# Transposed maxima in the bank of the value products, and a latent softmax that is normalised behind its product with the values

## The reference, cut to what matters

```python
h = layernorm(x) * (1 + ca) + sa
q, k, v = split(h @ qkv_w + qkv_b)                 # 16 heads of 16
local = window_attention(q, k, v)                  # the 128 tokens before, softmax
pooled = h.reshape(B, 64, 16, D).mean(2)           # 64 latents, chunks of 16 tokens
rk, rv = split(pooled @ rkv_w + rkv_b)             # 4 latent heads of 16
lattn = softmax((h @ rq_w + rq_b) . rk / 4 over earlier chunks)   # 0 where there are none
remote = (lattn . rv) @ rout_w + rout_b
gate = sigmoid(local @ gl_w + remote @ gr_w)
x = x + ga * ((gate * local + (1 - gate) * remote) @ out_w + out_b)
```

## Time and profile before

| | us |
|---|---|
| median of 3 runs | 580.47 |
| lowest and highest | 572.05, 580.49 |
| the profiled execution's own time | 576.64 |
| its span, first to last instruction | 574.9 |

### The profile page before, as it was taken

One profiled execution on the slowest core, in us unless ns is written; L12 is line 12 of the kernel. 1 busy time (PEld: TensorE's weight loads), 2 busy tenths in 40 slices (PEclk: granted clock), 3 DMA queues, 4 the chain that ended last, 5 costly groups with the idle time before them and its releaser, 6 DMA issues.

```text
span 574.9 us, 19855 instructions
## 1 busy us (share of the span) xinstructions
PE 482.9 (84%) x7168; PEld 364.1 (63%) x7168; DVE 436.6 (76%) x1193; ACT 353.8 (62%) x868; POOL 379.2 (66%) x516
## 2 busy tenths in 40 slices
PE   2446689999899999999999999999999999988771
PEld 2205567777677666777777676777776676766451
DVE  2155657788688888988988788888888887878554
ACT  1210466677677667777777577777776776766540
POOL 2222346778577767788877587777777677766663
PEclk9975889999899999999999899999999999999776
DMA  9558644618244444434252607162534444440000
GB/s 277 114 133 246 163 105 99 132 47 187 56 113 75 95 94 93 94 90 93 64 101 68 119 34 145 39 125 62 120 68 97 92 94 93 82 79 10 11 10 19
DMA packets 56523, 55.15 MB, mean 96 GB/s; under 512 B 7380, under 2 KB 53100, under 8 KB 54892
## 3 DMA queue, kind: packets, MB, share of 16 engines
q1 hardware_dynamic: 53564, 52.57, 41.4%
q10 hardware_dynamic: 2864, 1.31, 1.1%
HBM read 37.07 MB, written 16.80 MB: 94 GB/s over the span
## 4 chain that ended last, share of the span: by engine, by line
PE 72%; issue 11%; POOL 5%; DVE 4%; DMA 2%; ACT 2%; ACTq 1%; SPq 1%; POOLq 0%; DVEq 0%
PE p_pv L819 9%; PE p_qkv L730 9%; PE p_qkv L740 6%; PE p_misc L886 6%; PE p_y L806 5%; PE p_x L785 5%; PE p_y L807 5%; PE p_x L778 4%; PE p_a L751 3%; PE p_qkv L860 3%; PE p_misc L869 2%; PE p_a L831 2%; PE p_a L716 2%; PE p_misc L877 2%; PE p_a L753 2%
## 5 line engine op out<-in xcount | busy, mean ns | idle before, releaser
L592 ACT ACTIVATE pr<-p_y 128x512 f32<-128x512 f32 x224 | 124.6, 595 | 55.8 <-PE p_y L807 52.9
L1159 DVE TENSOR_REDUCE mtok<-p_x 128x3 bf16<-128x480 f32 (+1 forms) x192 | 109.3, 585 | 30.9 <-PE p_x L785 29.6
L441 POOL TENSOR_SCALAR_AFFINE_SELECT pr<-pr 128x512 f32<-128x512 f32 x128 | 89.6, 701 | 11.2 <-ACT pr L594 9.0
L451 POOL TENSOR_TENSOR rstd<-ve,half 128x1 f32<-128x1 f32 x96 | 58.1, 605 | 47.9 <-DVE ve L1079 47.7
L469 POOL TENSOR_TENSOR dif<-local,rem 128x272 f32<-128x272 f32 x32 | 30.9, 965 | 83.8 <-DVE local L1197 83.8
L445 POOL TENSOR_SCALAR_AFFINE_SELECT pr<-pr 128x512 f32<-128x512 f32 x112 | 81.3, 726 | 0.0
L807 PE MATMUL p_y<-qst,kst 112*128 112x128 bf16 x512 | 73.2, 221 | 0.0
L806 PE MATMUL p_y<-qst,kst 112*128 112x128 bf16 x448 | 66.5, 221 | 7.7 <-ACT pr L592 4.8
L819 PE MATMUL p_pv<-pr,vp 128*18 128x128 f32 x1920 | 67.1, 279 | 2.1 <-POOL pr L445 0.8
L730 PE MATMUL p_qkv<-hT,wqk 128*128 128x256 f32 x256 | 66.1, 403 | 2.2 <-DVE qkf L1111 1.3
L740 PE MATMUL p_qkv<-wv,hT 128*128 128x272 f32 x128 | 40.1, 439 | 29.5 <-issue 29.4
(11 more groups left out here) (131 smaller groups left out, 1092.7 us busy)
## 6 DMA issues: line engine op xcount, KB each, us to landing
scr_q<-terms SPq DMA_DIRECT2D x16, 384.0 KB, 2.5
qst<-scr_q SPq DMA_DIRECT2D x16, 384.0 KB, 4.7
scr_k<-terms SPq DMA_DIRECT2D x16, 384.0 KB, 4.4
kst<-scr_k SPq DMA_DIRECT2D x16, 384.0 KB, 5.4
qst<-scr_q SPq DMA_DIRECT2D x16, 256.0 KB, 5.4
kst<-scr_k SPq DMA_DIRECT2D x16, 256.0 KB, 6.4
out_y<-y SPq DMA_DIRECT2D x32, 128.0 KB, 1.7
x_all<-in_x SPq DMA_DIRECT2D x3, 1024.0 KB, 8.3
```

Of the source, the lines that this page charges most:

```text
L441: ins = pool.affine_select(out=own, in_=own, compare_op=ALU.is_ge, fill=0.0, base=-1, pattern=[[0, 4], [1, P]], channel_multiplier=-1)
L592: act.activation(pr[:, 2 * i:2 * i + 2, :, :], src, ACT.Exp).then_inc(exp_done[i], 1)
L1159: dve.tensor_reduce(mtok[:, KS + h0:KS + h1], p_x[i % 2][:, 0:(h1 - h0) * w].rearrange("p (h n) -> p h n", n=w), AX_X, ALU.max, negate=Tru ...
```

## The change

- The transposed maxima go into the bank `p_pv` instead of `p_qkv`. `max_t(m)` waits for `out_t(c)`, which reads that bank, and stands behind `scores(t, 1)`. `project_v` and `lat_remote` no longer wait for `shift`.
- ACT's order becomes `out_t`, `part1`, `shift`, `part2`, `lat_exp`; `lat_oT` is gone.
- The latents' exponentials are no longer summed or scaled ahead of their transposition. The operand of the values, `bvd` (and a second tile `bvd1` for tiles that see half the latents), holds ones in 64 more columns, so that `lat_out_t` leaves the sums in partitions 64 to 127 of `p_misc`. DVE takes their reciprocal (64x128) and multiplies; both stand behind `norm1(a)`, ahead of `maxima(t, 3)`. For the first tile of a batch one more small operation sets the 16 tokens without latents to zero.
- The old `lat_recip` (128x4) and `lat_norm` (128x256 or 128x128) on DVE are gone. The setup has four more copies on DVE.

```diff
@@ act
-                act.activation(q_of(t)[KS:KS + H, :, :], p_qkv[KS:KS + H, 0:P // 2].bitcast(BF16)...
+                act.activation(q_of(t)[KS:KS + H, :, :], p_pv[KS:KS + H, 0:P // 2].bitcast(BF16)...
             def lat_exp(t):
-                act.wait_ge(lp_ready, done(t - 1))
+                act.wait_ge(lpT_psum, done(t - 1))
                 for h in range(LH):
-                    ins = act.activation(by_head(le, t)[:, h, :], by_head(p_a, t)[:, h, :], ACT.Exp, bias=lneg[:, h:h + 1],
-                                         accum_out=lsum[:, h:h + 1])
+                    ins = act.activation(by_head(le, t)[:, h, :], by_head(p_a, t)[:, h, :], ACT.Exp, bias=lneg[:, h:h + 1])
-            def lat_oT(t):
-                act.wait_ge(loT_psum, done(t))
-                act.wait_ge(rem_psum, done(t - 1))
-                act.activation(loT[0:LD, :], p_misc[0:LD, 0:P], ACT.Copy).then_inc(loT_ready, 1)
             def slot(t, stages):
-                if Q:
-                    part1(r)
                 if C:
                     out_t(c)
                 if Q:
+                    part1(r)
+                if T:
+                    shift(m)
+                if Q:
                     part2(r)
-                if T:
-                    shift(m)
-                    lat_oT(m)
@@ pe
             def project_v(t):
-                pe.wait_ge(shift_ready, done(t - 2))
+                pe.wait_ge(rem_ready, done(t - 3))
             def max_t(t):
-                pe.wait_ge(qk_copied, done(t + 3))
-                pe.wait_ge(rem_ready, done(t - 1))
-                pe.transpose(p_qkv[:, 0:P // 2].bitcast(BF16), mtok[:, :], ident_bf[:, :]).then_inc(mT_psum, 1)
+                pe.wait_ge(oT_ready, done(t - 1))
+                pe.transpose(p_pv[:, 0:P // 2].bitcast(BF16), mtok[:, :], ident_bf[:, :]).then_inc(mT_psum, 1)
             def lat_p_t(t):
-                pe.wait_ge(lp_ready, done(t))
+                pe.wait_ge(lexp_ready, done(t))
...
-                    ins = pe.transpose(p_a[:, k * P:(k + 1) * P], lp[:, k * P:(k + 1) * P], ident)
+                    ins = pe.transpose(p_a[:, k * P:(k + 1) * P], le[:, k * P:(k + 1) * P], ident)
             def lat_out_t(t):
-                    ins = pe.matmul(p_misc[:, 0:P], bvd[:, t % 2, k, :], lpT[:, k * P:(k + 1) * P],
+                    ins = pe.matmul(p_misc[:, 0:P], values_of(t)[:, k, :], lpT[:, k * P:(k + 1) * P],
             def lat_remote(t):
-                pe.wait_ge(shift_ready, done(t))
             def slot(t, stages):
+                if S:
+                    scores(t, 1)
                 if T:
                     max_t(m)
                 if S:
-                    scores(t, 1)
                     scores(t, 0)
@@ dve
+                      *[dve.tensor_copy(bvd[:, r, :, LD:2 * LD], cst[:, C_RV:C_RV + 2 * LD].rearrange("p (k l) -> p k l", k=2))
+                        for r in range(2)],
+                      *[dve.tensor_copy(bvd1[:, r, LD:2 * LD], cst[:, C_RV1:C_RV1 + LD]) for r in range(2)],
             def lat_recip(t):
+                dve.wait_ge(loT_psum, done(t))
+                dve.reciprocal(rden[:, :], p_misc[LD:2 * LD, 0:P]).then_inc(rden_ready, 1)
             def lat_norm(t):
+                dve.wait_ge(rden_ready, done(t))
+                dve.wait_ge(rem_psum, done(t - 1))
                 if t % NB:
+                    dve.tensor_tensor(loT[0:LD, :], p_misc[0:LD, 0:P], rden[:, :], ALU.mult).then_inc(loT_ready, 1)
                 else:
+                    dve.tensor_scalar(loT[0:LD, 0:CH], rden[:, 0:CH], 0.0, None, ALU.mult)
+                    dve.tensor_tensor(loT[0:LD, CH:P], p_misc[0:LD, CH:P], rden[:, CH:P], ALU.mult).then_inc(loT_ready, 1)
             def slot(t, stages):
                 if A:
                     norm1(a)
+                if T:
+                    lat_recip(m)
+                    lat_norm(m)
                 if S:
                     maxima(t, 3)
...
-                if S:
-                    lat_recip(t)
...
-                if S:
-                    lat_norm(t)
```

More of the change, by code:

```diff
@@ L50 @@
 SU_SILU, SU_MODT, SU_ROWS = 3, 9, 22
-SU_PRE = SU_ROWS + 13
+SU_PRE = SU_ROWS + 17
 SU_ALL = SU_PRE + B // 2
@@ L62 @@
 C_IND = C_RV1 + LD
-C_VAL = C_IND + P
-C_BRK = C_VAL + 1
+C_BRK = C_IND + P
 C_BD = C_BRK + 1
@@ L139, in build @@
         bvd = sb("bvd", [P, 2, 2, P])
+        bvd1 = sb("bvd1", [P, 2, P])
         mtok = sb("mtok", [P, P], BF16)
@@ L144, in build @@
         le = sb("le", [P, LH * LT])
[L145 to L148, removed]
+        rden = sb("rden", [LD, P])
         lpT = sb("lpT", [P, 2 * P])
@@ L221, in build @@
         ls_psum, lmx_ready, lexp_ready = counted("ls_psum", "PE"), counted("lmx_ready", "DVE"), counted("lexp_ready", "ACT")
-        lval_ready, lp_ready = counted("lval_ready", "DVE"), counted("lp_ready", "DVE")
-        lrec_ready = sem("lrec_ready")
+        rden_ready = counted("rden_ready", "DVE")
         lpT_psum, lpT_ready = counted("lpT_psum", "PE"), counted("lpT_ready", "ACT")
-        loT_psum, loT_ready = counted("loT_psum", "PE"), counted("loT_ready", "ACT")
+        loT_psum, loT_ready = counted("loT_psum", "PE"), counted("loT_ready", "DVE")
         rem_psum, rem_ready = counted("rem_psum", "PE"), counted("rem_ready", "ACT")
@@ L262, in seen, with values_of @@
             return LT // 2 if t % NB < NB // 2 else LT
+        def values_of(t):
+            return bvd[:, t % 2, :, :] if seen(t) == LT else bvd1[:, t % 2:t % 2 + 1, :]
         def by_head(ap, t):
@@ L582, in shift @@
                 act.wait_ge(st_psum[LAST_ST], done(t - 4))
-                act.activation(q_of(t)[KS:KS + H, :, :], p_qkv[KS:KS + H, 0:P // 2].bitcast(BF16).unsqueeze(1).to_broadcast([H, H, P]),
+                act.activation(q_of(t)[KS:KS + H, :, :], p_pv[KS:KS + H, 0:P // 2].bitcast(BF16).unsqueeze(1).to_broadcast([H, H, P]),
                                ACT.Copy).then_inc(shift_ready, 1)
@@ L647, in slot @@
                 if Q:
-                    part2(r)
+                    part1(r)
                 if T:
                     shift(m)
-                    lat_oT(m)
+                if Q:
+                    part2(r)
                 if S:
@@ L1146, in spread_rv @@
                 if seen(t) < LT:
-                    ins = dve.tensor_tensor(bvd[:, t % 2, 0, 0:LD], rvb[:, :], cst[:, C_RV1:C_RV1 + LD], ALU.mult)
+                    ins = dve.tensor_tensor(bvd1[:, t % 2, 0:LD], rvb[:, :], cst[:, C_RV1:C_RV1 + LD], ALU.mult)
                 else:
@@ L1168, in lat_recip, with lat_norm @@
             def lat_recip(t):
-                dve.wait_ge(lexp_ready, done(t))
+                dve.wait_ge(loT_psum, done(t))
+                dve.reciprocal(rden[:, :], p_misc[LD:2 * LD, 0:P]).then_inc(rden_ready, 1)
+            def lat_norm(t):
+                dve.wait_ge(rden_ready, done(t))
+                dve.wait_ge(rem_psum, done(t - 1))
                 if t % NB:
-                    dve.reciprocal(lrec[:, :], lsum[:, :]).then_inc(lval_ready, 1)
+                    dve.tensor_tensor(loT[0:LD, :], p_misc[0:LD, 0:P], rden[:, :], ALU.mult).then_inc(loT_ready, 1)
                 else:
-                    dve.reciprocal(lrec2[:, :], lsum[:, :]).then_inc(lrec_ready, NB)
-                    dve.wait_ge(lrec_ready, t + NB)
-                    dve.tensor_scalar(lrec[:, :], lrec2[:, :], cst[:, C_VAL:C_VAL + 1], None, ALU.mult).then_inc(lval_ready, 1)
-            def lat_norm(t):
-                dve.wait_ge(lval_ready, done(t))
-                dve.wait_ge(lpT_psum, done(t - 1))
-                dve.tensor_tensor(by_head(lp, t), by_head(le, t), bc(lrec[:, :], seen(t)), ALU.mult).then_inc(lp_ready, 1)
+                    dve.tensor_scalar(loT[0:LD, 0:CH], rden[:, 0:CH], 0.0, None, ALU.mult)
+                    dve.tensor_tensor(loT[0:LD, CH:P], p_misc[0:LD, CH:P], rden[:, CH:P], ALU.mult).then_inc(loT_ready, 1)
             def prob_sum(t):
@@ L1391, in constants @@
         c[LD + q, C_IND + q * CH:C_IND + (q + 1) * CH] = 1
-    c[CH:, C_VAL] = 1
     c[LD:LD + CPB, C_BRK] = 1
```

## The result

| | before | after |
|---|---|---|
| median of 4 runs, us | 578.85 | 597.44 |
| lowest and highest, us | 572.05, 580.49 | 592.76, 598.34 |
| profiled execution, us | 576.64 | 596.93 |
| its span, us | 574.9 | 595.2 |

The ratio is 1.033 with a 95% interval of 1.022 to 1.043: slower, as forecast, and inside the range. The forecast was 604, so the loss came out at 20.3 us between the profiled executions (18.6 between the medians) where 28 was predicted.

The account below looks back on a forecast made before the run. The prediction took a slot loop through `out_tokens`, `local_out`, `difference` and POOL's masks to bound the kernel. 26 slots at +0.95 us (24.7), +3, +1 and -0.7 made +28 on 576.64, so 604; range 586 to 620.

Parts of the forecast that it names:

- the forecast path from part1 over `res1` and `rstd1`: In ACT, POOL and DVE: part1 queued behind `out_t` delays `res1`, `rstd1` (end 3.04) and `norm1` (3.12 instead of 2.37).
- the 3.3 us put beside the loop: Outside the 26 full slots: last slots +3, setup copies +1, the slot held by the load of x -0.7 us.
- the delay of a slot: From `out_t` to `difference`: late `norm1`, reciprocal and product lengthen each of 26 slots by 0.95 us, 24.7 in all.
- the cheap rival: DVE's reciprocal at one element a cycle, 0.33 us: `prob_sum` 0.28 late, +10 us, 587; chance 0.13.
- The row-by-row slope of 7.1 ns an element: DVE's reciprocal, from rows of 253 ns for 16 elements and 168 for 4: estimated 1.05 us for 128.
- POOL's unbroken chain: From `difference` to the last mask POOL works without a gap, 7.65 us, and sets the slot's pace.
- The 27 waits of 0.38 us: Ahead of the last value products: PE was said to wait 27 times, 0.38 us each, for POOL's mask of L445.
- The stack of k, costed at nothing with a rival beside it: k's stack load behind the later `part3`: forecast 0; rival, 13 odd slots of 17.4 us, +13.4, 618, chance 0.10.
- The rival that had PE's stall count: Before the value projection: removing PE's wait saves 0.65 us in 26 slots, -17, giving 560; chance 0.05.

Follow-up runs that it names:

- The mask left out: The changed kernel with one of POOL's eight masks left out (previous tile's keys, second group of heads): 594.48 us, ratio to before 1.031.
- both halves ordered: The changed kernel with ACT's old order, `max_t` behind `lat_scores`, two `mtok` buffers and q's load ahead of the store of the result: 567.06 us, 0.982.
- bank alone: The kernel before with the maxima in `p_pv` and the new orders of PE and ACT, latents as before: 594.82 us, 1.031.
- copy: The changed kernel with a copy in place of DVE's reciprocal, the product kept: 590.46 us, ratio to before 1.024.
- part1 first with `max_t` later: The changed kernel with part1 ahead of `out_t`, `max_t` behind `lat_scores` and two `mtok` buffers, `part2` still behind `shift`: 599.9 us, 1.036.
- ordered bank: The kernel before with maxima in `p_pv`, ACT's order kept, `max_t` behind `lat_scores`, two `mtok` buffers: 573.83 us; with q's load ahead of the store, 556.88.

## Why the prediction was right, and what was off

The direction and the place were right. The value projection has no idle; PE's idle moved to `out_tokens`; the delay stands ahead of `norm1` and in the reciprocal, and with `max_t` moved the forecast path from part1 over `res1` and `rstd1` gives `norm1` at 2.91 by itself; from `difference` to the next `out_t` it was 9.4 us, before and after. The total is closer than its parts: the slots were delayed by half of what was forecast, and single slots lost some 5 us more than the 3.3 us put beside the loop. That these two errors have opposite signs is luck.

**The mis-sized term: the delay of a slot**, 0.95 forecast, 0.43 to 0.49 measured, so about 12 us of 26 slots instead of 24.7. The error is spread over the chain of steps that the prediction wrote down. `rstd1` ended at 2.87, not 3.04 (`res1` took 1.16, not 1.27); `norm1` took 0.40 beside an idle POOL, not 0.60; the reciprocal 0.96, not 1.05; the product 0.28, not 0.33. Each is small and all have one sign; with the gaps between them they make 0.37 us at `out_tokens` (4.75, not 5.12) and 0.5 at `difference`. The chain was estimated link by link, and each link was put too high; in a loop that runs 26 times 0.1 us is 2.6.
The Trainium skill ("VectorE: DVE Perf Modes", "First, the fixed hardware budget") has the reciprocal as an iterative divide with a repeat count of 8. Read as eight cycles an element that is an estimate of 1.07 us plus a start; the trace has 0.96 in all, which is less than that reading, though nearer to it than to the 0.33 of the cheap rival. The row-by-row slope of 7.1 ns an element turned out at (959 - 253) / 112 = 6.3.

**The step that was wrong: POOL's unbroken chain sets the slot.** The mask left out refutes it for ordinary slots. A row of the page of before spoke against it already. The 27 waits of 0.38 us that the prediction gave to PE are those of PEld, PE's weight loads, which overlap its products; the products themselves waited 0.8 us in all for that mask:

```profile
L819 PE MATMUL p_pv<-pr,vp 128*18 128x128 f32 x1920 | 67.1, 279 | 2.1 <-POOL pr L445 0.8
```

In the table slot 13 is `out_tokens` + 11.1 in eleven of the fourteen kernels (before 11.06, after 11.09, both halves ordered 11.08), and where POOL comes late to `difference` it is `difference` + 9.0 to 9.2 (bank alone 9.06, copy 9.22, part1 first with `max_t` later 9.04), whichever is later. In before PE's path was the later one by 0.2 to 0.3 us (5.99 + 9.1 against 15.39). The forecast did not suffer, because the change moved both by the same 0.4 to 0.5.

**The step that was missing:** `max_t` behind `out_t` holds not only PE but, through the one buffer of `mtok`, DVE's `maxima(t, 1)`, and that puts `norm1` at the same place as `rstd1` does. The prediction priced that wait for PE alone. This is why undoing part1 by itself recovers only 6 us, nearly none of it in slots with all latents, and moving `max_t` alone nothing.

**The stack of k, costed at nothing with a rival beside it,** did cost. The store landed in 2.6 us as forecast, but with `part3` at 4.90 the slack is gone: PE's waits ahead of the first scores, 2.3 us in slot 2 and 1.3 in the longer slot 24, are such. In the variants the place of q's load ahead of k's store decides the total (ordered bank 573.8 or 556.9), by the waits themselves and by the lower clock that stood behind the longest of them. The rest of the 20.3 us lies in single slots: the half-clock stretch of slot 9, the extra operation of first tiles behind the late `norm1`, which the sum passed over, and the last five slots, 3.1 us, where 3 was forecast. Some 2 us in slot 3, an idle of PE before the last value products, stay open; why a lower clock falls in slot 9 in one kernel and slot 17 in the other stays open too.

The rival that had PE's stall count was wrong for the change as it was made. Its price was near, though: the bank's half takes 0.74 us from an ordinary slot (15.39 to 14.65) with ACT's order as it was and `mtok` doubled, and that reaches the total only with q's load out of the way of k's store.

## What to carry to other kernels

When a wait is taken away by moving an instruction, follow its producers on every engine: here the bank's half gains 0.74 us a slot in a good order, and the reorder of ACT and one single-buffered tile gave back more than that. If undoing one cause changes nothing, two waits may end together; take both away in one run before dropping either. A loop that gets shorter meets the next fixed period, here a pair of stack loads, whose store landed late while another load was under way on the same queue.

## What the runs showed of the hardware beside that

A reciprocal of 128 elements a partition takes 959 ns where a copy of the same tile out of the bank takes 293.

Some operations of DVE were about twice as long beside a busy POOL. `norm1` took 0.82 us in slot 15 of before, beside `add_u` and `add_bias` (`part3` had just ended), and 0.40 in the kernel after with POOL idle. Not every operation is: the reciprocal out of the bank took 0.96 us in all its 32 runs of the kernel after, beside `part3` or not. The write of the latents' values, which the change left alone but for its columns, stands beside POOL's masks (L445) now, where in before it stood beside the one-column `rstd` of L451. The groups of before, and of after:

```profile
L607 ACT ACTIVATION_READ_ACCUMULATOR le<-p_a,lneg 128x1 f32 x128 | 25.3, 198 | 0.0
...
L1149 DVE TENSOR_TENSOR bvd<-rvb,cst 128x128 f32<-128x128 f32 x16 | 4.5, 279 | 0.0
```

```profile
L1144 DVE TENSOR_TENSOR bvd<-rvb,cst 128x128 f32<-128x128 f32 x16 | 11.4, 715 | 0.0
```

That neighbour is a likely cause of the 279 and 715 ns, not one tested by itself. The first line is the sum that an exponential returns: an instruction of its own, 198 ns, 25.3 us of ACT in all. Nothing shows that taking it out gave time: ACT's exponentials wait for PE in both kernels, and no run takes it out alone.

A store of 384 KB (k's terms) issued while the load of q's stack was still under way on the same queue took 4.4 us to land; with that load issued earlier it took 2.5.
